# Written-out orders, one-pass scores, and tokens placed pair by pair in a gated cross-attention and routed-FFN kernel

## The chip, the cores and the metric

The kernel runs on one core of one Trainium2 chip. The metric is the device time of one execution in microseconds; lower is better. PE is TensorE, PEld its weight loads, DVE is VectorE, ACT is ScalarE, POOL is GpSimd, SP is SyncE, which here only issues DMAs.

## The reference

`x` is 8 batches of 256 tokens of width 256, the context is 8 batches of 77 keys of width 192. All data are fp32.

```python
# attention, 16 heads of 16
q = layernorm(x) @ wq + bq ; k = y @ wk + bk ; v = y @ wv + bv
out = softmax(q k^T / sqrt(16)) v  @ wo + bo
x = x + tanh(g_xattn) * out
# feed-forward on xf = layernorm(x)
top1 = argmax(softmax(xf @ gate_w.T))            # one of 2 experts per token
h = relu(einsum('end,edh->enh', masked, w1) + b1)  # masked: xf where chosen, else 0
routing_output = (einsum('enh,ehd->end', h, w2) + b2).sum(experts)
shared = relu(xf @ sw1 + sb1) @ sw2 + sb2        # hidden 1024
x = x + tanh(g_ffn) * (routing_output + shared)
```

A token that an expert was not chosen for still adds relu(b1) @ w2 + b2 of that expert: the kernel calls this row `other_row`.

## The kernel before, in words

**Arithmetic.** Most products are made in three fp32r matmuls (`cut`, line 1110 on): each operand is split into a part `hi` that fp32r holds and a rest `lo`, and hi·hi, lo·hi and hi·lo are accumulated. ACT writes `hi` from PSUM, and DVE (for weights in part POOL) writes `lo` as the difference. Scores, values and the product with the probabilities are plain fp32 matmuls, which the trace shows as two records each.

**Attention of one batch** (256 tokens, two groups of 8 heads). `in`: PE transposes the normalised rows `xn` to `xnT`. `query`: 12 fp32r matmuls of 256 columns. `scores`: four quarters (a tile of 128 tokens by a group); each is two fp32 matmuls of 308 columns against `k_diag`, a block-diagonal matrix in which SP has set each head's keys with a DMA of its own (line 409, 8 per batch). `soft`: DVE takes the maxima over 77 keys and subtracts them, in two halves; `exp` is ACT's, `sums` DVE's sum and reciprocal, and POOL multiplies (line 582). `turn`: 20 transposes of the probabilities. `values`: 10 fp32 products with the block-diagonal `v_diag`, which SP fills with 12 small DMAs per batch from DRAM (line 416). `out`: 12 fp32r matmuls; DVE adds to `x_all` and takes the statistics of the second layer norm.

**Shared layers of a pair of batches** (512 tokens). `norm2` transposes the normalised rows, `gate` and `gate_turn` give the two gate scores. For each of 8 chunks of the hidden width, `h` is 6 matmuls of 512 columns, evicted twice by ACT (`hT_hi`, and `h32` from which DVE makes `hT_lo`, line 1006), and `y` is 12 matmuls of 256 columns that accumulate in `y_ps`.

**Order.** `START`, `ORDER` and `END` (lines 86 to 124) list steps (name, pair offset, batch of the pair, k); every engine walks the same list and does its own part of each step. `START` serves pair 0, a hardware loop does `ORDER` for pairs 1 and 2, `END` pair 3. The shared layers of pair i-1 stand among the attention of pair i; those of pair 3 come last. SP has its own program: loads, diagonals, `fill` of `sorted_dram` with 10 DMAs of empty rows (line 477), expert weights.

**Routing.** After the last gate, `count`, `choose` and `sort` give each of the 2048 tokens a row of `sorted_dram`, expert 0 from the front and expert 1 behind a seam at a multiple of 256. POOL then issues 16 indirect DMAs (line 612), one for each 128 tokens. `other` (line 1332) makes `other_row`, 24 matmuls per expert. SP loads the first 256 sorted rows, PE transposes them (line 1340), and nine routed tiles follow in a loop: 8 hidden chunks and 8 output chunks each, a gather of the shared result from `part_dram`, and two scatters to `out`.

The matmuls of `cut` and `mm` all bear line 1114 in the trace.

## Time and profile before

| | us |
|---|---|
| median of 3 runs | 403.01 |
| lowest, highest | 402.02, 403.04 |
| span of the profiled execution | 400.4 |
| PE busy | 355.8 (89%) |
| DVE busy | 241.8 (60%) |
| ACT busy | 186.7 (47%) |
| POOL busy | 162.4 (41%) |
| mean granted TensorE clock | 0.972 |

The profile shows one execution, from its first to its last instruction; no device time is given for that execution by itself, so its span stands beside the three runs. A matmul's own length in the trace contains its way through the array, and neighbours overlap; how far apart two start is what one costs. Several operations share a helper's line, so the tile names tell more than the lines.

### The profile page before, as it was taken

Reading aid. Unit: us, or ns where it says so; the run is one execution under the profiler, and the core shown is the slowest. Engines: PE = TensorE matmul, PEld = TensorE weight load, DVE = VectorE, ACT = ScalarE, POOL = GpSimd, SP = SyncE. Lnnn points to the kernel's source line nnn. Section 1 sums busy time; section 2 is a strip of 40 time slices with the busy share of each in tenths; the row PEclk is TensorE's granted clock in tenths of the full one; section 3 lists DMA queues with packets and bytes.
Section 4 is the critical chain, followed back from the end, with each engine's and each line's share of the span. In section 5 each row is a group of like instructions: output and inputs, shape, how many; then the busy total and the mean of one; then the engine's idle time right before and its main releaser. Section 6 shows DMA issues by size and latency. Waiting matters only on the chain. (4 is left out here: it accounts for less than half of the span.)

```text
span 400.4 us, 7423 instructions
## 1 busy us (share of the span) xinstructions
PE 355.8 (89%) x2341; PEld 313.7 (78%) x2341; DVE 241.8 (60%) x592; ACT 186.7 (47%) x398; POOL 162.4 (41%) x164
## 2 busy tenths in 40 slices
PE   3697868799999999999999999963999999999990
PEld 3475756577889878889868988853999999999990
DVE  0789897669758979668784377640244444445440
ACT  3323544265654346635247238610555456546550
POOL 8132365541612412615026042871244455444452
PEclk9989998999999999999999999995899999999997
DMA  6810170059500030000300012723211222221120
GB/s 157 262 25 10 37 237 12 8 148 249 149 9 11 3 108 12 9 4 4 106 2 0 2 54 58 283 94 118 52 50 43 66 79 69 58 64 43 61 63 10
DMA packets 34541, 28.31 MB, mean 71 GB/s; under 512 B 15562, under 2 KB 32073, under 8 KB 34521
## 3 DMA queue, kind: packets, MB, share of 16 engines
q1 hardware_dynamic: 31737, 21.16, 19.3%
q0 software_dynamic: 2784, 6.91, 5.5%
q8 instruction: 10, 0.16, 0.2%
q14 instruction: 10, 0.08, 0.1%
HBM read 16.02 MB, written 9.82 MB: 65 GB/s over the span
## 5 line engine op out<-in xcount | busy, mean ns | idle before, releaser
L1006 DVE TENSOR_TENSOR hT_lo<-h,hT_hi 128x256 fp32r<-128x256 f32 (+1 forms) x104 | 57.5, 555 | 65.5 <-ACT h L686 60.7
L582 POOL TENSOR_TENSOR probs<-probs,rinv 128x616 f32<-128x616 f32 x32 | 40.9, 1282 | 111.9 <-DVE rinv L902 111.9
L683 ACT ACTIVATE hT_hi<-h_ps,vec_cols 128x256 fp32r<-128x256 f32 (+1 forms) x68 | 39.2, 577 | 61.8 <-PE h_ps L1114 55.7
L753 ACT ACTIVATE probs<-probs 128x616 f32<-128x616 f32 x32 | 23.0, 720 | 53.0 <-DVE probs L953 53.0
L1114 PE MATMUL bank<-k_diag,qT 128*128 128x308 f32 x128 | 39.8, 434 | 3.0 <-ACT qT L700 2.2
L1114 PE MATMUL y_ps<-ew_hi,hT_hi 128*128 128x256 f32 x144 | 42.1, 292 | 0.0
L1114 PE MATMUL y_ps<-ew_hi,hT_lo 128*128 128x256 f32 x144 | 40.3, 280 | 0.0
L1114 PE MATMUL y_ps<-ew_lo,hT_hi 128*128 128x256 f32 x144 | 40.2, 280 | 0.0
L1114 PE MATMUL y_ps<-sw_hi,hT_hi 128*128 128x256 f32 x128 | 38.2, 299 | 1.8 <-DVE hT_lo L1006 1.6
L686 ACT ACTIVATE h<-h_ps,vec_cols 128x256 f32<-128x256 f32 (+1 forms) x68 | 39.0, 574 | 0.0
L1114 PE MATMUL bank<-pT,v_diag 128*128 128x256 f32 (+1 forms) x160 | 36.0, 380 | 0.6 <-ACT pT L723 0.5
L1114 PE MATMUL y_ps<-sw_hi,hT_lo 128*128 128x256 f32 x128 | 36.1, 282 | 0.0
L1114 PE MATMUL y_ps<-sw_lo,hT_hi 128*128 128x256 f32 x128 | 36.1, 282 | 0.0
L1114 PEld LDWEIGHTS bank<-pT,v_diag 128*128 128x128 f32 (+1 forms) x160 | 30.2, 190 | 5.9 <-issue 1.5
L645 POOL DMA_INDIRECT out<-final,scatter_token x18 | 18.9, 1050 | 34.3 <-DVE final L1099 21.1
L944 DVE TENSOR_REDUCE smax<-bank 128x4 f32<-128x308 f32 x64 | 27.9, 469 | 6.9 <-PE bank L1114 6.7
L1114 PEld LDWEIGHTS bank<-k_diag,qT 128*128 128x128 f32 x128 | 22.9, 193 | 9.6 <-ACT qT L700 2.4
L723 ACT ACTIVATE pT<-bank 128x256 f32<-128x256 f32 (+1 forms) x80 | 24.6, 389 | 10.9 <-PE bank L1211 10.9
L1114 PE MATMUL h_ps<-x2T_hi,sw_hi 128*128 128x512 f32 x64 | 27.2, 424 | 0.5 <-ACT h L686 0.5
L1114 PEld LDWEIGHTS y_ps<-ew_hi,hT_hi 128*128 128x128 f32 x144 | 27.1, 188 | 0.6 <-DVE hT_lo L1006 0.2
L953 DVE TENSOR_TENSOR probs<-bank,smax 128x308 f32<-128x308 f32 x64 | 27.4, 470 | 0.1
L1114 PEld LDWEIGHTS y_ps<-ew_lo,hT_hi 128*128 128x128 f32 x144 | 27.2, 189 | 0.0
(168 smaller groups left out, 958.4 us busy)
## 6 DMA issues: line engine op xcount, KB each, us to landing
stage<-in_L_ffn_w SPq DMA_DIRECT2D x4, 1024.0 KB
sorted_dram<-empty_rows SPq DMA_DIRECT2D x10, 257.0 KB, 4.7
xs<-sorted_dram SPq DMA_DIRECT2D x10, 257.0 KB
stage<-in_L_ffn_sw SPq DMA_DIRECT2D x2, 1024.0 KB
xn_all<-xn SPq DMA_DIRECT2D x4, 512.0 KB, 3.7
part_dram<-x_all SPq DMA_DIRECT2D x4, 512.0 KB, 3.0
x_all<-in_x SPq DMA_DIRECT2D x2, 512.0 KB, 9.1
x_all<-in_x SPq DMA_DIRECT2D x1, 1024.0 KB, 12.8
```

Of the source, the lines that this page charges most:

```text
L582: nc.gpsimd.tensor_tensor(pq, pq, rinv[:, b, k, :].unsqueeze(2).to_broadcast([P, HG, KEYS]), ALU.mult).then_inc(p_ready, 1)
L645: pool.indirect_dma_start(out=out[:, :], out_offset=bass.IndirectOffsetOnAxis(ap=scatter_token[:, t:t + 1], axis=0), in_=final[:, t, :], i ...
L683: nc.scalar.activation(hT[0][:, c % HB, 0:width], hidden_bank(c % banks)[:, 0:width], ACT.Relu, bias=b1_sb[:, m, c:c + 1]).then_inc(h_hi, 1)
L686: nc.scalar.activation(h32[:, c % 2, 0:width], hidden_bank(c % banks)[:, 0:width], ACT.Relu, bias=b1_sb[:, m, c:c + 1]).then_inc(h_32, 1)
L723: nc.scalar.activation(pT[0:r, 2 * u + v, :], bank[2 + u % 2][0:r, v * SEQ:(v + 1) * SEQ], ACT.Copy).then_inc(pT_sb, 1)
L753: nc.scalar.activation(probs[:, b, k, :], probs[:, b, k, :], ACT.Exp, scale=HEAD_DIM ** -0.5).then_inc(p_exp, 1)
L944: nc.vector.tensor_reduce(out=smax[:, b, k, half * HH:(half + 1) * HH], in_=by_head(bank[half][:, 0:HALF]), axis=AX_X, op=ALU.max).then_in ...
L953: nc.vector.tensor_tensor(by_head(probs[:, b, k, half * HALF:(half + 1) * HALF]), by_head(bank[half][:, 0:HALF]), m, ALU.subtract).then_in ...
L1006: nc.vector.tensor_tensor(hT[1][:, c % HB, 0:width], h32[:, c % 2, 0:width], hT[0][:, c % HB, 0:width], ALU.subtract).then_inc(h_lo, 1)
L1114: return nc.tensor.matmul(out_, lhsT, rhs, start=start, stop=stop, **kw)
```

## The change

1. The four lists are replaced by five, one for each engine, with every step of all eight batches written out (no loop over pairs). `n` in `tn.b.u.m` and the like: batch (or unit of two batches), part, PSUM bank.
2. Scores of batches 1 to 7 are made with fp32r in one matmul per stack of two heads: the contraction of 128 rows is [q hi; q lo; q hi; q lo] of two heads (32 rows each) against [k hi; k hi; k lo; k lo], block-diagonal over the two heads, 154 columns; four matmuls per quarter. `q_parts` goes to DRAM and comes back in four pieces, the keys in eight. Batch 0 still uses fp32 against a `k_diag`, now made by DVE. Maxima and shift are one DVE instruction per quarter each.
3. `v_diag` is written as rows into a zeroed DRAM image (2 DMAs per batch) and read back whole (2 DMAs, 0.63 MB).
4. Normalising of both layer norms moves from DVE to ACT (`scale`, `bias`), with one more DVE instruction in each root. The `lo` parts of q, k and of 5 of 8 hidden chunks move to POOL.
5. Tokens are placed and scattered per unit of two batches: expert 0 from the front, expert 1 from the back (`flip`), with a running count. POOL issues the scatters of a unit (4) when its places are known.
6. Both `other` products, and the first transposes of sorted rows, stand among the last shared chunks. The bias of the shared layer is added once to `other_row`, and no longer to each row of `x_all`. `fill` comes early on SP.

```diff
-ORDER = [("scores", 0, 1, 0), ("soft", 0, 1, 0), ("exp", 0, 1, 0), ("values", 0, 0, 0), ("norm2", -1, 0, 0),
-         ("scores", 0, 1, 1), ("norm2", -1, 0, 1), ("soft", 0, 1, 1), ("exp", 0, 1, 1), ("norm", 1, 0, 0),
-         ("out", 0, 0, 0), ("gate", -1, 0, 0), ("h", -1, 0, 0), ("scores", 0, 1, 2), ("gate_turn", -1, 0, 0),
...
-CUT_AFTER = {1: (0, 0), 2: (0, 1), 4: (1, 0), 6: (1, 1)}
+LO_ON_POOL = (1, 2, 4, 5, 6)
+PE_ORDER = """
+    yt.0 yt.1 yt.2 yt.3 vt kp.0.0 kp.0.1 kp.1.0 kp.1.1 vp.0 in.0.0 vp.1 vp.2 qy.0.1 in.1.0 vp.3 sc.0.0 qy.1.1
+    sc.0.1 sc.0.2 in.2.0 tn.0.0.1 sc.0.3 tn.0.1.0 qy.2.1 in.3.0 sc.1.0 tn.0.2.1 tn.0.3.0 tn.0.4.1 qy.3.0 sc.1.1
+    in.4.1 sc.1.2 va.0.0 tn.1.0.1 sc.1.3 tn.1.1.1 ou.0.0 sc.2.0 qy.4.1 in.5.0 sc.2.1 tn.1.2.1 tn.1.3.0 tn.1.4.1
+    qy.5.0 sc.2.2 va.1.1 tn.2.0.0 sc.2.3 tn.2.1.0 in.6.1 ou.1.0 qy.6.1 sc.3.0 tn.2.2.0 tn.2.3.1 tn.2.4.0 sc.3.1
+    in.7.1 va.2.0 n2.0.0.1 sc.3.2 n2.0.1.0 qy.7.1 sc.3.3 tn.3.0.0 h.0.0 tn.3.1.0 ga.0.1 sc.4.0 ou.2.0 gt.0.1
+    h.0.1 h.0.2 tn.3.2.1 tn.3.3.0 sc.4.1 h.0.3 tn.3.4.1 ct.0.0 sc.4.2 y.0.0 va.3.1 sc.4.3 h.0.4 tn.4.0.0
+    tn.4.1.1 y.0.1 ou.3.0 sc.5.0 h.0.5 tn.4.2.1 tn.4.3.0 y.0.2 tn.4.4.1 sc.5.1 h.0.6 va.4.0 sc.5.2 y.0.3
+    tn.5.0.1 tn.5.1.0 h.0.7 n2.1.0.1 n2.1.1.0 sc.5.3 y.0.4 y.0.5 ou.4.1 sc.6.0 h.1.0 ga.1.0 tn.5.2.1 h.1.1
+    gt.1.0 tn.5.3.1 sc.6.1 y.0.6 tn.5.4.0 ct.1.1 h.1.2 sc.6.2 va.5.0 sc.6.3 y.0.7 tn.6.0.1 tn.6.1.0 h.1.3 ou.5.1
+    sc.7.0 y.1.0 tn.6.2.0 h.1.4 tn.6.3.1 tn.6.4.0 sc.7.1 y.1.1 va.6.1 sc.7.2 h.1.5 tn.7.0.0 ou.6.1 sc.7.3
+    tn.7.1.0 y.1.2 h.1.6 y.1.3 h.1.7 n2.2.0.1 n2.2.1.0 y.1.4 y.1.5 oth.0.1 h.2.0 tn.7.2.0 h.2.1 y.1.6 tn.7.3.0
+    h.2.2 tn.7.4.0 y.1.7 h.2.3 va.7.0 y.2.0 h.2.4 ou.7.0 y.2.1 h.2.5 ga.2.0 y.2.2 h.2.6 gt.2.0 y.2.3 h.2.7
+    ct.2.0 oth.1.1 n2.3.0.0 y.2.4 n2.3.1.1 y.2.5 y.2.6 h.3.0 ga.3.0 h.3.1 gt.3.1 h.3.2 y.2.7 ct.3.0 h.3.3 y.3.0
+    h.3.4 y.3.1 h.3.5 y.3.2 h.3.6 y.3.3 h.3.7 xst.1 y.3.4 y.3.5 y.3.6 y.3.7
+"""
+POOL_ORDER = """
+    klo.0.0 klo.0.1 bi.0 klo.1.0 va_.0 klo.1.1 bi.1 va_.1 ql.1 di.0.0 bi.2 di.0.1 bi.3 bi.4 di.0.2 di.0.3 ql.2
+    bi.5 di.1.0 ql.3 bi.6 di.1.1 va_.2 di.1.2 di.1.3 bi.7 ql.4 di.2.0 di.2.1 va_.3 ql.5 di.2.2 di.2.3 ql.6
+    di.3.0 di.3.1 di.3.2 ql.7 di.3.3 hl.1 di.4.0 hl.2 scat.0 di.4.1 di.4.2 hl.4 di.4.3 hl.5 di.5.0 hl.6 di.5.1
+    di.5.2 di.5.3 di.6.0 hl.9 scat.1 di.6.1 hl.10 di.6.2 di.6.3 hl.12 di.7.0 di.7.1 hl.13 di.7.2 hl.14 di.7.3
+    hl.17 hl.18 hl.20 wl.5 hl.21 hl.22 scat.2 hl.25 hl.26 scat.3 hl.28 hl.29 hl.30
+"""
+SP_ORDER = """
+    vz kw.0 kw.1 kr.1 qw.1 fl qr.1 vw.0 wd.0 wd.1 kr.2 qw.2 vr.0 vw.1 qr.2 wd.2 wd.3 qw.3 vr.1 vw.2 qr.3 kr.3
+    vr.2 vw.3 qw.4 vw.4 vr.3 qr.4 qw.5 kr.4 qw.6 vw.5 vr.4 qr.5 kr.5 qw.7 vw.6 vr.5 qr.6 kr.6 vw.7 vr.6 qr.7
+    kr.7 vr.7 ps.0 wd.4 wd.5 ps.1 ps.2 xs ps.3
+"""
...
+            def keys_in(b):
+                n = b % 2
+                if b == 1:
+                    sp.wait_ge(cleared[0], 1)
+                else:
+                    sp.wait_ge(s_ready, 4 * (b - 1))
+                sp.wait_ge(k_out[b // 4], 16 * 2 * STACKS)
+                for piece in range(4):
+                    for h in range(2):
+                        to = slice(piece * SR + h * HEAD_DIM, piece * SR + (h + 1) * HEAD_DIM)
+                        sp.dma_start(k_stack[to, n, :, :, h, :].rearrange("r i g n -> r (i g) n").bitcast(F32),
+                                     k_dram[h * HEAD_DIM:(h + 1) * HEAD_DIM, piece // 2, :, :,
+                                            b * KEYS:(b + 1) * KEYS].rearrange("r i g n -> r (i g) n")
+                                     ).then_inc(k_in[n], 16)
+            def queries_out(b):
+                sp.wait_ge(q_hi, b + 1)
+                sp.wait_ge(q_lo, b)
+                if b >= 3:
+                    sp.wait_ge(q_in[b % 2], 16 * 4 * ((b - 1) // 2))
+                sp.dma_start(q_dram[b % 2].rearrange("m p g s -> p m (g s)"),
+                             q_parts[:, :, :, :].rearrange("p m g s -> p m (g s)").bitcast(F32)
+                             ).then_inc(q_out[b % 2], 16)
+            def queries_in(b):
+                n = b % 2
+                if b >= 2:
+                    sp.wait_ge(s_ready, 4 * (b - 1))
+                sp.wait_ge(q_out[n], 16 * ((b + 1) // 2))
+                for piece in range(4):
+                    sp.dma_start(q_stack[piece * SR:(piece + 1) * SR, n, :, :, :].rearrange("r i g s -> r i (g s)"
+                                                                                            ).bitcast(F32),
+                                 q_dram[n, piece % 2].rearrange("(i r) g s -> r i (g s)", i=STACKS)
+                                 ).then_inc(q_in[n], 16)
+            def values_out(b):
+                n = b % 2
+                sp.wait_ge(v_rdy, b // 2 + 1)
+                if b < 2:
+                    sp.wait_ge(v_zeroed, 16 * 4)
+                else:
+                    sp.wait_ge(v_in[n], 16 * 2 * (b // 2))
+                for g in range(GROUPS):
+                    diagonal = bass.AP(v_rows, n * GK * GROUPS * P + g * P,
+                                       [[GROUPS * P, KEYS], [KEYS * GROUPS * P + HEAD_DIM, HG], [1, HEAD_DIM]])
+                    sp.dma_start(diagonal, v32[:, (b // 2) % 2, n, g * P:(g + 1) * P].rearrange("k (h f) -> k h f", h=HG)
+                                 ).then_inc(v_out[n], 16)
+            def values_in(b):
+                n = b % 2
+                sp.wait_ge(v_out[n], 16 * GROUPS * (b // 2 + 1))
+                if b < 2:
+                    sp.wait_ge(v_zeroed, 16 * 4)
+                else:
+                    sp.wait_ge(o_ps, b - 1)
+                full = CHUNKS - 1
+                sp.dma_start(v_diag[:, n, 0:full, :, :].rearrange("p c g f -> p c (g f)"),
+                             v_dram[n, 0:full * P].rearrange("(c p) g f -> p c (g f)", p=P)).then_inc(v_in[n], 16)
+                sp.dma_start(v_diag[0:ROWS[full], n, full, :, :].rearrange("p g f -> p (g f)"),
+                             v_dram[n, full * P:GK].rearrange("p g f -> p (g f)")).then_inc(v_in[n], 16)
...
+            def queries_lo(b):
+                pool.wait_ge(q_32, b)
+                pool.wait_ge(q_hi, b + 1)
+                if b >= 2:
+                    pool.wait_ge(q_out[(b - 1) % 2], 16 * (b // 2))
+                nc.gpsimd.tensor_tensor(q_parts[:, 1, :, :].rearrange("p g s -> p (g s)"),
+                                        q32[:, :, :].rearrange("p g s -> p (g s)"),
+                                        q_parts[:, 0, :, :].rearrange("p g s -> p (g s)"), ALU.subtract
+                                        ).then_inc(q_lo, 1)
...
+            def scatter(u):
+                n, tiles = u % 2, UNIT_TILES[u]
+                pool.wait_ge(numbers_made, 2)
+                if u == 0:
+                    pool.wait_ge(k_lo, 2 * GROUPS)
+                if u >= 2:
+                    pool.wait_ge(scattered[n], 16 * TILES_AS[u])
+                nc.gpsimd.tensor_copy(xn2[:, n, 0:tiles, DIM:ROW].rearrange("p t o -> p (t o)"),
+                                      number[:, TILE0[u]:TILE0[u] + tiles]).then_inc(tokens_put, 1)
+                if u == 0:
+                    pool.wait_ge(filled, 16 * (RTILES + 1))
+                pool.wait_ge(tokens_put, u + 1)
+                pool.wait_ge(xn2_ready, u + 1)
+                pool.wait_ge(places_rdy, u + 1)
+                for t in range(tiles):
+                    pool.indirect_dma_start(
+                        out=sorted_dram[:, :], out_offset=bass.IndirectOffsetOnAxis(ap=place_int[:, n, t:t + 1], axis=0),
+                        in_=xn2[:, n, t, :], in_offset=None, bounds_check=SLOTS - 1,
+                        oob_is_err=False).then_inc(scattered[n], 16)
...
+            nc.gpsimd.memset(part[:, :, :], 0.0).then_inc(part_clear, 1)
+            pool.wait_ge(other_scaled, 1)
+            nc.gpsimd.tensor_tensor(other_row[:, :, :], other_row[:, :, :],
+                                    bias_rows[:, 1, :].unsqueeze(1).to_broadcast([P, EXPERTS, DIM]), ALU.add
+                                    ).then_inc(other_rdy, 1)
...
-                            dve.wait_ge(s_ps, quarter * 2 + half + 1)
-                            nc.vector.tensor_reduce(
-                                out=smax[:, b, k, half * HH:(half + 1) * HH], in_=by_head(bank[half][:, 0:HALF]),
-                                axis=AX_X, op=ALU.max).then_inc(s_max, 1)
+            def maxima(b, k):
+                dve.wait_ge(s_ready, 4 * b + k + 1)
+                nc.vector.tensor_reduce(out=smax[:, b % 2, k, :].rearrange("p (n h) -> p n h", n=2), in_=score_heads(),
+                                        axis=AX_X, op=ALU.max).then_inc(s_max, 1)
+            def shifted(b, k):
+                if b == 1 and k == 0:
+                    dve.wait_ge(k_out[0], 16 * 2 * STACKS)
+                    dve.wait_ge(k_out[1], 16 * 2 * STACKS)
+                if b >= 2:
+                    dve.wait_ge(pT_ps, TURNS * (b - 1))
+                dve.wait_ge(s_max, 4 * b + k + 1)
+                m = smax[:, b % 2, k, :].rearrange("p (n h) -> p n h", n=2).unsqueeze(3).to_broadcast([P, 2, HH, KEYS])
+                nc.vector.tensor_tensor(probs[:, b % 2, k, :].rearrange("p (n h k) -> p n h k", n=2, k=KEYS),
+                                        score_heads(), m, ALU.subtract).then_inc(s_shifted, 1)
...
+                dve.wait_ge(rank_step, 5 * u + 3)
+                dve.wait_ge(counts_ps, u + 1)
+                nc.vector.tensor_tensor_scan(running[:, 1:tiles + 1], bank[m][:, 128:128 + tiles], zero_tile[:, 0:tiles],
+                                             running[:, 0:1], ALU.add, ALU.add).then_inc(rank_step, 1)
+                dve.wait_ge(rank_step, 5 * u + 4)
+                nc.vector.tensor_tensor(rank1[:, 0:tiles], bank[m][:, 64:64 + tiles], running[:, 0:tiles], ALU.add
+                                        ).then_inc(rank_step, 1)
+                dve.wait_ge(rank_step, 5 * u + 5)
+                if u >= 2:
+                    dve.wait_ge(scattered[u % 2], 16 * TILES_AS[u])
+                nc.vector.tensor_tensor(place_int[:, u % 2, 0:tiles], slot0[:, 0:tiles], rank1[:, 0:tiles], ALU.subtract
+                                        ).then_inc(places_rdy, 1)
...
+            let_go = [None, (vecs_rdy, 1)]
+            def fill_bank(m, sem_, count):
+                if let_go[m]:
+                    pe.wait_ge(*let_go[m])
+                let_go[m] = (sem_, count)
...
-                        for half in range(2):
-                            if not early or (b, k) != (0, 0):
-                                pe.wait_ge(s_shifted, quarter * 2 - 1 + half)
-                            mm(bank[half][:, 0:HALF], qT[:, b, g, t * P:(t + 1) * P],
-                               k_diag[:, b, g, half * HALF:(half + 1) * HALF], True, True).then_inc(s_ps, 1)
+            def scores(b, k):
+                t, g = k % TB, k // TB
+                quarter = 4 * b + k
+                if quarter == 0:
+                    pe.wait_ge(yT_sb, 2)
+                    pe.wait_ge(q_hi, 1)
+                else:
+                    pe.wait_ge(s_shifted, quarter)
+                if b == 0:
+                    pe.wait_ge(k_diag_rdy, g + 1)
+                    for half in range(2):
+                        ins = mm(s_ps[:, half, 0:HALF], qT[:, g, t * P:(t + 1) * P],
+                                 k_diag[:, g, half * HH:(half + 1) * HH, :].rearrange("p h k -> p (h k)"), True, True)
+                else:
+                    if k == 0:
+                        pe.wait_ge(q_in[b % 2], 16 * 4 * ((b + 1) // 2))
+                        pe.wait_ge(k_in[b % 2], 16 * 8 * ((b + 1) // 2))
+                    for i in range(STACKS):
+                        ins = mm(s_ps[:, i // 2, i % 2 * SK:(i % 2 + 1) * SK],
+                                 q_stack[:, b % 2, i, g, t * P:(t + 1) * P],
+                                 k_stack[:, b % 2, i, g, :, :].rearrange("p h k -> p (h k)"), True, True)
+                ins.then_inc(s_ready, 1)
...
+            def other(e, m):
+                if e == 0:
+                    fill_bank(m, other_scaled, 1)
+                pe.wait_ge(rb_cut, 1)
+                pe.wait_ge(w_lo[3 + 2 * e], 1)
+                for c in range(HC):
+                    ins = cut(bank[m][:, e * DIM:(e + 1) * DIM],
+                              lambda n: relu_b1p[n][:, e, c:c + 1].to_broadcast([P, P]),
+                              lambda n: ew2_sb[e][n][:, c, :], c == 0, c == HC - 1)
+                ins.then_inc(other_ps, 1)
...
+                if step == "xst":
+                    fill_bank(at[0], xsT_lo, 1)
+                    sorted_turn(0, *at)
+            pe.wait_ge(w_lo[2], 1)
+            pe.wait_ge(w_lo[4], 1)
+            pe.wait_ge(other_scaled, 1)
+            pe.wait_ge(y_out, len(UNITS))
+            pe.wait_ge(h_32, CHUNKS_SHARED)
+            pe.wait_ge(seam_rdy, 1)
+            tiles_of_0 = pe.value_load(tiles0_int[0:1, 0:1], min_val=1, max_val=RTILES - 1)
```

## Rows read from the trace of the kernel before

**Rows 1.** Stretches: length, busy of PE, PEld, DVE, ACT, POOL, clock, DMA share, GB/s
```profile
24.39:92.49 68.10, 57.13 (x299) 43.53 (x298) 54.47 (x157) 28.42 (x59) 31.77 (x26) 0.97 0.30 79
92.49:265.09 172.60, 168.77 (x1036) 144.61 (x1034) 124.74 (x278) 88.57 (x168) 61.70 (x55) 1.00 0.21 60
265.09:283.07 17.98, 8.69 (x56) 8.49 (x55) 2.10 (x3) 0.60 (x1) 5.84 (x6) 0.72 0.31 96
283.07:400.40 117.33, 106.95 (x901) 106.11 (x899) 48.97 (x108) 61.38 (x154) 52.32 (x54) 0.98 0.19 56
```

**Rows 2.** Timeline of SP, its DMA issues: start, us, what
```profile
27.57 20.05 SPq L416 DMA_DIRECT2D v_diag<-values_dram  x24
84.69 6.86 SPq L477 DMA_DIRECT2D sorted_dram<-empty_rows  x10
93.95 1.95 SPq L409 DMA_DIRECT2D k_diag<-kT  x1
```

**Rows 3.** Timeline of PE in the beginning: start, us, what
```profile
19.65 0.55 PE L1114 MATMUL bank<-xnT_hi,wqo_hi 128*128 128x256 f32 x1 [3.74 <-DVE xnT_lo L868]
24.39 1.20 PE L1114 MATMUL bank<-k_diag,qT 128*128 128x308 f32 x4
25.43 1.89 PE L1114 MATMUL h_ps<-wv_sb,yT 96*77 96x256 f32 x8
47.47 4.56 PE L1114 MATMUL bank<-pT,v_diag 128*128 128x256 f32 x20
87.84 1.20 PE L1114 MATMUL bank<-k_diag,qT 128*128 128x308 f32 x4
```

**Rows 4.** Timeline of POOL, first and last of 16 scatters
```profile
247.13 2.74 POOL L612 DMA_INDIRECT sorted_dram<-xn_all,place_int  x1 [8.97 <-issue]
271.74 0.97 POOL L612 DMA_INDIRECT sorted_dram<-xn_all,place_int  x1 [0.30 <-issue]
```

**Rows 5.** The chain that ended last, in order of time
```profile
271.74 2.53 DMA sorted_dram<-xn_all,place_int
274.28 2.96 DMA xs<-sorted_dram
278.40 4.68 PE bank L1114 x24
```

**Rows 6.** Timeline of PE and of DVE at the end of the shared layers
```profile
265.09 0.28 PE L1114 MATMUL bank<-ew_hi,relu_b_hi 128*128 128x256 f32 x1
265.20 0.28 PE L1114 MATMUL bank<-ew_hi,relu_b_lo 128*128 128x256 f32 x1
265.29 1.41 DVE L1015 SCALAR_TENSOR_TENSOR x_all<-y_ps,gains,x_all 128x512 f32<-128x512 f32 x2 [1.78 <-PE y_ps L1114]
```

**Rows 7.** Timeline of PE, paces in the middle of the kernel
```profile
101.37 0.40 PE L1114 MATMUL h_ps<-x2T_hi,sw_lo 128*128 128x512 f32 x1
101.61 0.39 PE L1114 MATMUL h_ps<-x2T_lo,sw_hi 128*128 128x512 f32 x1
107.86 1.04 PE L1211 MATMUL bank<-ident,probs 128*128 128x128 f32 x8
149.47 0.40 PE L1259 MATMUL bank<-ident,gate_rows 2*128 2x2 f32 x4
```

**Rows 8.** Groups of instructions, shapes apart: busy, mean ns, idle before
```profile
L944 DVE TENSOR_REDUCE smax<-bank 128x4 f32<-128x308 f32 x64 | 27.9, 469 | 6.9 <-PE bank L1114 6.7
L899 DVE TENSOR_REDUCE rsum<-probs 128x8 f32<-128x616 f32 x32 | 25.0, 782 | 2.7 <-ACT probs L753 2.7
L902 DVE RECIPROCAL rinv<-rsum 128x8 f32<-128x8 f32 x32 | 6.5, 203 | 1.1
L582 POOL TENSOR_TENSOR probs<-probs,rinv 128x616 f32<-128x616 f32 x32 | 40.9, 1282 | 111.9 <-DVE rinv L902 111.9
L639 POOL TENSOR_TENSOR part<-part,other_row 128x256 f32<-128x256 f32 x18 | 14.9, 846 | 15.9 <-DMA part<-part_dram,gather_token 15.9
```

**Rows 9.** DMA issues: KB each, median us to landing
```profile
xn_all<-xn SPq DMA_DIRECT2D x4, 512.0 KB, 3.7
```

1638 lines of the change are left out of this document (877 added, 761 removed), and 7 rows, old and new, of the table END.

## The prediction, made before the changed kernel ran

> **What bounds it now.** I cut the span at the events of TensorE: the first shared hidden matmul (92.49), the first matmul of `other` (265.09) and the routed part (283.07) [rows 1]. Before 92.5 us TensorE is not the limit: DVE is busy 54.5 of the 68.1 us after the first scores, and SP spends 20.05 us on issuing the 24 pieces of `v_diag`; the first product with `v_diag` (47.47) starts as that ends [rows 1 to 3]. From 92.5 to 265.1 TensorE is busy 168.8 of 172.6 us: there only less work for it helps. From 265.1 to 283.1 it mostly waits. The chain of waits runs through POOL, whose 16 scatters go from 247.13 to 272.7, their landing (2.53), the load of `xs` (2.96), and a cold half of `other`: 24 matmuls in 4.68, at a mean clock of 0.72 in this stretch, against 0.117 apart warm [rows 1, 4 to 6]. From 283.1 on nine routed tiles fill TensorE.
>
> **Paces, warm.** What a matmul costs is the distance to the next one, not its own length. fp32r: 256 columns 0.117 us, 512 columns 0.24; a transpose (1.04 - 0.28)/7 = 0.11 [rows 6, 7]. An fp32 product of 308 columns is two records, and a quarter (two products) goes from 24.39 to 25.43: 1.04 us. The 20 records with `v_diag` are (4.56 - 0.38)/19 = 0.22 apart, 4.4 a batch [rows 3].
>
> **Part 1, scores in one pass.** No row has an fp32r matmul of 154 columns. The line through 256 and 512 columns gives 0.07 us, four per quarter 0.29: 0.75 less than 1.04. The other end is that narrow ones run at the fp32 price per column, 4 x 154 x 1.04/616 = 1.04, and save nothing. I take 0.29, since that line passes near zero, and keep 1.04 for a rival. Loading the weights could be a floor, but `gate_turn` loads 128 columns four times with its matmuls (0.40 - 0.20)/3 = 0.07 us apart [rows 7]. The Trainium skill ("TensorE: Matmul & The Clock Gate", LDWEIGHTS) puts such a load at its columns over 1.2 GHz, 107 ns; the row speaks against that as a distance, and by the rule a quarter would cost 0.43 and the sum come out 2.2 us higher.
>
> DVE now takes the maxima of a quarter in one instruction, not two: 2 x 0.469 become about 0.82 (the 616-wide sum takes 0.782); the shift I price the same. A quarter is 0.82 + 0.82 + 0.78 + 0.20, with gaps 2.8 us [rows 8]. The price is a detour. Per batch ACT evicts the queries twice, POOL subtracts (512 wide: 1.1 us, between 0.85 for 256 and 1.28 for 616), SP writes 512 KB (3.7 to landing, by `xn_all`), reads 1 MB back in four pieces and the keys in eight; the values cost 4 issues instead of 12. At 20.05/24 = 0.84 an issue, 17 replace 20 [rows 2, 8, 9]. Behind 92 us I cost the detour at nothing: between qy.5 and sc.5.0 TensorE has over 30 us of other work. In the beginning it has no such cover.
>
> **Part 2, the beginning.** (a) All four value steps precede the first scores: 24 fp32 records more, 5.3 us, of which the idle 3.74 before `xnT_lo` hides most. Scores start near 26, not 24.39 [rows 3]. (b) Batch 0, still fp32: four times about 3.0, and 4 us for the second root and three `xnT_lo`: 42. (c) Batch 1 needs its stack. qy.1 ends near 29, ACT 2.6, POOL 1.1, qw.1 0.7: 33.5. The ten fills come next on SP: 6.86 us of issues, 2.57 MB, and the queue is slow until 94, 9.3 us after they begin [rows 2]. qr.1 reads its 1 MB behind them: 47. (d) va.0 stands before sc.1.3 and needs vr.0, which SP reaches behind wd.0 and wd.1 (2 MB, at the fills' rate 6.5 to 7.5), kr.2 and qw.2 (5 together), with 0.63 MB of its own (2): 61. With va.0's 4.4 and the last quarter batch 1 ends at 68. (e) Batch 2: 11.2 + 1.4 (two `xnT_lo`) + 0.7 (`oT_lo`) + 1.5 (`x1`, statistics) = 14.8: 83. Batch 3: the same with 2.6 for the root, less its tail: 98. So h.0.0 starts at 98 where it was 92.49. Bounds: 88 if the waits of (c) and (d) are half as long, 112 if each also delays the next stack.
>
> **Part 3, the full stretch.** By 92.49 the old kernel has done half of batch 3's scores [rows 3] and the queries of four batches. At h.0.0 the new order has done two quarters more (2.1), four `in` and `qy` more (4 x 1.84 = 7.4, from 12 x 0.117 and 4 x 0.11) and four transposes (0.4), and lacks ou.2 and ga.0 (2 x 1.4): 7.1 ahead. Of 172.6 remain 172.6 - 7.1 - 16 quarters x 0.75 (12.0) + 5.6 for both `oth` (48 x 0.117), which move in here: 159.1. A check from below: 32 x (6 x 0.23 + 12 x 0.117) = 89 for h and y, scores 4.6, transposes 10, va 21.7, ou 8.4, gates and x2T 9.3, oth 5.6: 149, and 5% for gaps: 157. The others stay below: DVE about 95 of 159 us; POOL takes 20 of 32 `hT_lo` (1.1 each) beside 16 divisions of 1.28 [rows 8]; ACT takes over the normalising, 0.5 a tile.
>
> **Part 4, the handover.** Twelve of sixteen scatters are now issued earlier, under matmuls; four are left after pl.3. From ct.3 to xst TensorE has five h and four y, 12.6 us. Against that: DVE's placing 1, POOL's four issues 5 to 6, landing 2.5, load 3.0 [rows 4, 5]: 12, so xst waits 0 to 1. After y.3.7 it waits for ad.3 (1.41, plus signals) [rows 6]. I take 2.5 for the stretch that took 17.98; cold `other` is gone with it. Four placings instead of one cost DVE some 4 us, beside matmuls.
>
> **Part 5, the routed tiles.** The same instructions per tile; the bias moved from `x_all` into `other_row`, once, under the handover. 117.3 stays [rows 1].
>
> **The sum.** 98 + 159.1 + 2.5 + 117.3 = 376.9 of span against 400.4. The median of the runs shown, 403.0, lies 2.6 above the profiled span; with it **379.5 us**.
>
> **Rivals.** (A) Narrow fp32r matmuls cost what fp32 does, so the change gives no one-pass time: 16 x 0.75 = 12.0 in part 3 (in the beginning it hides under DVE's 0.98 of sums): 391.5. For: no row under 256 columns. Against: the straight line. (B) The beginning is as quick as DVE allows, h.0.0 at 88: 369.5. For: before the stretch SP's queue was its limit, and it issues less. Against: the fills now come early. (C) The last scatters come late: the first of a group takes 2.74, not 0.97 [rows 4], POOL arrives late from its `hT_lo`, TensorE cools: +6, 385.5. (D) Slower than before: SP's single order. Reads of values wait for a va two batches earlier, and stack reads stand behind them. If sc.b.0 or va.b waits t in batches 3 to 7, it costs 5t; above t = 4.7 the time passes 403. With 7, what (d) exposes at batch 1, it is 414.5. For: the fills show a queue full for 9 us [rows 2]; the Trainium skill ("DMA: Bandwidth & Descriptors", Queues, rings and completion order) has each ring consume its descriptors in order. Against: later TensorE has matmuls between, and no block of 2.5 MB follows.
>
> **Chances.** Forecast (own range 371 to 388) 0.50; A 0.25; B 0.12; C 0.06; D 0.05; a mixture near no change 0.02. The range goes from B's side, 366, to A with a late beginning, 397; beyond lie D and the far ends. Within 0.3%, about what a measurement of this kernel cannot tell from no change: 0.02; faster 0.93, slower 0.05.
>
> **What would show it.** Score matmuls 0.07 apart (A: 0.26). The first h at 98, with TensorE's waits before it at sc.1.0 behind the queries' DMA and at va.0 behind the values'. From there to the routed part 162. No wait on `xs` over 1 us; scatters in four groups. Routed part 117. I am wrong if TensorE waits over 10 us in the middle stretch, or if the routed tiles change.

## The result, and the profile after

| | before | after |
|---|---|---|
| median of 4 runs, us | 403.02 | 413.39 |
| lowest, highest | 402.02, 403.10 | 412.10, 415.53 |
| span of the profiled execution | 400.4 | 411.0 |
| mean granted TensorE clock | 0.972 | 0.936 |

The ratio is 1.026, with a 95% interval of 1.022 to 1.030: the change made the kernel slower, where 379.5 us and faster were forecast, and outside the forecast's range of 371 to 388.

The stretches of after, cut at TensorE's first scores, the first stacked scores (`sc.1.0`), the first shared hidden matmul (`h.0.0`) and the routed part (length; busy of PE, PEld, DVE, ACT, POOL; clock; DMA share; GB/s):

```profile
0.00:32.72 32.72, 18.30 (x85) 13.55 (x86) 19.27 (x56) 12.39 (x27) 19.41 (x40) 1.00 0.64 184
32.72:60.47 27.75, 11.74 (x57) 8.17 (x56) 14.88 (x45) 11.74 (x24) 14.83 (x17) 0.77 0.89 193
60.47:123.89 63.42, 50.56 (x273) 44.29 (x273) 42.67 (x77) 34.53 (x63) 23.40 (x22) 0.80 0.84 227
123.89:292.32 168.43, 158.91 (x1043) 141.31 (x1042) 101.47 (x206) 87.89 (x147) 76.61 (x62) 0.99 0.31 78
292.32:411.00 118.68, 107.94 (x900) 107.57 (x900) 48.33 (x108) 61.07 (x153) 52.71 (x54) 0.95 0.20 58
```

Against [rows 1]: from `h.0.0` to the routed part 168.4 us for 190.6 (172.60 + 17.98). There the change does what it is for, and 22.2 us are saved; by the prediction's own count (an estimate) 7.1 of them are work that the new order has only moved ahead of `h.0.0`. But `h.0.0` comes at 123.9 for 92.5, 31.4 us later. The routed part takes 1.4 more. In the beginning the granted clock is 0.77 and 0.80 where it was 0.97, and the DMA engines, idle for 70% of that stretch before, are busy for 84 to 89%.

TensorE in the beginning of after (timeline; four of the six rows from `sc.1.0` to `h.0.0` that have a wait over 1 us ahead of them, in square brackets, and one quarter at full clock with what follows it; the other two waits, 1.28 and 1.89 us, are for VectorE's shift):

```profile
60.47 1.11 PE L1361 MATMUL s_ps<-k_stack,q_stack 128*128 128x154 f32 x4 [11.67 <-issue]
73.00 7.22 PE L1361 MATMUL bank<-pT,v_diag 128*128 128x256 f32 x20 [4.17 <-issue]
83.32 0.57 PE L1361 MATMUL s_ps<-k_stack,q_stack 128*128 128x154 f32 x4
83.72 0.32 PE L1361 MATMUL bank<-xnT_hi,wqo_hi 128*128 128x256 f32 x1
101.15 0.66 PE L1479 MATMUL bank<-ident,probs 128*128 128x128 f32 x4 [1.61 <-ACT q_parts L857]
111.13 1.15 PE L1479 MATMUL bank<-ident,probs 128*128 128x128 f32 x8 [2.06 <-ACT q_parts L857]
```

The values of batch 0, 4.56 us for 20 records before [rows 3], take 7.22: in their first 5 us the granted clock is 0.50, half of full speed. SP's issues around the two long waits:

```profile
35.74 4.77 SPq L451 DMA_DIRECT2D k_stack<-k_dram  x8
40.60 0.38 SPq L462 DMA_DIRECT2D q_dram<-q_parts  x1
41.02 7.46 SPq L526 DMA_DIRECT2D sorted_dram<-empty_rows  x10
48.53 2.53 SPq L473 DMA_DIRECT2D q_stack<-q_dram  x4
51.16 2.52 SPq L489 DMA_DIRECT2D v_rows<-v  x2
53.78 6.19 SPq L518 DMA_DIRECT2D stage<-in_L_ffn_sw  x2
```

and the landings of the queries that stand in the chain of waits:

```profile
64.37 6.05 DMA q_dram<-q_parts
74.29 10.94 DMA q_dram<-q_parts
95.15 5.00 DMA q_dram<-q_parts
104.08 6.04 DMA q_dram<-q_parts
```

`qe` is ScalarE's eviction of a batch's queries into `q_parts`. There is one `q_parts` for all batches, so the next `qe` waits for each of these landings, and what is queued behind `qe` on ScalarE holds TensorE's banks: that is the releaser `ACT q_parts` above. The late start has another source (ScalarE's timeline):

```profile
8.20 0.42 ACT L787 ACTIVATE pT<-s_ps 96x308 f32<-96x308 f32 x1 [2.76 <-PE s_ps L1384]
15.16 0.20 ACT L977 ACTIVATE gains<-gains 128x2 f32<-128x2 f32 x1 [6.54 <-DMA h<-in_L_ffn_b]
15.27 0.40 ACT L787 ACTIVATE pT<-s_ps 96x308 f32<-96x308 f32 x1
```

The tanh is second in `ACT_ORDER` and waits for the expert biases, which take 10.2 us to land; three evictions of the turned context, from which the keys are made, stand behind it.

### The profile page after: what moved, and what is told of

Its sections match the earlier page's. It is cut to its first block, busy times and chain, and to the rows that moved or that the text cites. A ratio compares the mean times of both kernels' runs of the same rounds, so it can differ in the third digit from the quotient of the medians.

```text
span 411.0 us, 7156 instructions
## 1 busy us (share of the span) xinstructions
PE 347.4 (85%) x2353; PEld 314.9 (77%) x2353; DVE 226.6 (55%) x490; ACT 207.6 (51%) x412; POOL 187.0 (45%) x194
## 4 chain that ended last, share of the span: by engine, by line
PE 52%; SPq 11%; DVE 10%; DMA 9%; POOL 6%; issue 6%; ACT 4%; POOLq 0%; DVEq 0%; ACTq 0%
PE y_ps L1361 20%; PE h_ps L1361 14%; PE s_ps L1361 7%; PE bank L1361 7%; DMA q_dram<-q_parts 7%; SPq L451 3%; SPq L473 3%; DMA h<-in_L_ffn_b 2%; PE bank L1479 2%; SPq L526 2%; SPq L518 2%; POOL sorted_dram L691 2%; POOL probs L672 1%; DVE rstd L1042 1%; DVE rsum L1161 1%
## 5 line engine op out<-in xcount | busy, mean ns | idle before, releaser
L1327 DVE TENSOR_TENSOR hT_lo<-h,hT_hi 128x256 fp32r<-128x256 f32 x72 | 32.7, 454 | 48.8 <-ACT h L1021 44.3
L700 POOL TENSOR_TENSOR hT_lo<-h,hT_hi 128x512 fp32r<-128x512 f32 x20 | 27.6, 1385 | 42.2 <-ACT h L935 42.0
L1018 ACT ACTIVATE hT_hi<-h_ps,vec_cols 128x256 fp32r<-128x256 f32 x36 | 17.1, 474 | 50.1 <-PE h_ps L1361 47.9
L930 ACT ACTIVATE hT_hi<-h_ps,vec_cols 128x512 fp32r<-128x512 f32 x32 | 21.9, 684 | 33.5 <-PE h_ps L1361 32.9
L1161 DVE TENSOR_REDUCE rsum<-probs 128x8 f32<-128x616 f32 x32 | 25.3, 789 | 20.4 <-ACT probs L864 19.6
L874 ACT ACTIVATE pT<-bank 128x512 f32<-128x512 f32 x40 | 23.4, 598 | 23.4 <-PE bank L1479 23.4
L1143 DVE TENSOR_REDUCE smax<-s_ps 128x8 f32<-128x616 f32 x32 | 24.9, 779 | 13.8 <-PE s_ps L1361 13.4
L1479 PE MATMUL bank<-ident,probs 128*128 128x128 f32 (+1 forms) x160 | 25.9, 300 | 7.6 <-ACT q_parts L857 3.7
L1361 PE MATMUL s_ps<-k_stack,q_stack 128*128 128x154 f32 x112 | 18.9, 293 | 14.8 <-issue 11.7
L1479 PEld LDWEIGHTS bank<-ident,probs 128*128 128x128 f32 (+1 forms) x160 | 19.7, 151 | 12.5 <-ACT q_parts L857 4.3
```

The costliest lines, as they stand in the source:

```text
L700: nc.gpsimd.tensor_tensor(hT[1][:, q % HB, 0:width], h32[:, q % 2, 0:width], hT[0][:, q % HB, 0:width], ALU.subtract).then_inc(h_lo_pool, 1)
L874: nc.scalar.activation(pT[:, 2 * u:2 * u + 2, :].rearrange("p c s -> p (c s)"), bank[m][:, :], ACT.Copy).then_inc(pT_sb, 1)
L930: nc.scalar.activation(hT[0][:, q % HB, 0:width], h_ps[:, q % 2, 0:width], ACT.Relu, bias=b1_sb[:, 0, c:c + 1]).then_inc(h_hi, 1)
L1018: nc.scalar.activation(hT[0][:, c % HB, 0:RTOK], hidden_bank(c % 4)[:, 0:RTOK], ACT.Relu, bias=b1_sb[:, 1 + e, c:c + 1]).then_inc(h_hi, 1)
L1143: nc.vector.tensor_reduce(out=smax[:, b % 2, k, :].rearrange("p (n h) -> p n h", n=2), in_=score_heads(), axis=AX_X, op=ALU.max).then_inc( ...
L1161: nc.vector.tensor_reduce(out=rsum[:, b % 2, k, :], in_=probs[:, b % 2, k, :].rearrange("p (h k) -> p h k", k=KEYS), axis=AX_X, op=ALU.add ...
```

## The experiments

Each group of kernels ran beside the kernel before on one chip; ratios are to that. Besides the ratio the table gives three points of each profile. `h.0.0` less `sc.1.0` is three batches; "middle" is from `h.0.0` to the routed part. A profile is one execution: `sc.1.0` differs by up to 2.4 us between kernels whose edits don't touch what stands ahead of it.

The expectations number their theories: (1) what stands ahead of the query stacks in SP's order, (2) the round trip of the queries through DRAM as such, (3) the late tanh, (4) VectorE's cut in the last root, (5) the cuts of the shared weights, (6) TensorE is the bound only behind `h.0.0`, (7) the low clock. Step names in the lists: on SP `kw`, `qw`, `vw` write keys, queries and values to DRAM, `kr`, `qr`, `vr` read them back, `fl` is the fills, `wd` a load of weights (0 and 1 shared, 2 and 3 the first expert's), `vz` the zeroing; `wh` and `wl` are ScalarE's and VectorE's parts of cutting weights, `ro` the steps of a reciprocal root, `ad` an addition of the shared result, `kb` matmuls without use, `sm`, `ss`, `su`, `ex` maxima, shift, sums and exponential of the scores, `te` the eviction of turned probabilities; on TensorE `in`, `qy`, `sc`, `tn`, `va`, `ou` are the steps of a batch's attention.

| kernel | ratio (95%) | `sc.1.0` | `h.0.0` | middle |
|---|---|---|---|---|
| after | 1.026 (1.022 to 1.030) | 60.5 | 123.9 | 168.4 |
| fills_late | 1.031 (1.028 to 1.035) | 50.2 | 125.1 | 169.9 |
| tanh_late | 1.017 (1.013 to 1.021) | 56.2 | 118.8 | 169.5 |
| experts_late | 1.025 (1.020 to 1.030) | 60.1 | 123.3 | 169.9 |
| no_detour3 | 1.011 (1.007 to 1.015) | 58.2 | 115.8 | 168.5 |
| fills_first | 1.000 (0.997 to 1.004) | 49.5 | 111.9 | 169.5 |
| cut_late | 1.015 (1.012 to 1.018) | 56.1 | 117.9 | 167.0 |
| pool_writes | 1.025 (1.022 to 1.028) | 56.0 | 119.3 | 171.1 |
| keys_merged | 1.014 (1.010 to 1.018) | 54.7 | 116.8 | 168.6 |
| combined | 0.995 (0.991 to 0.999) | 50.4 | 111.9 | 167.4 |
| shared_cut_later | 0.996 (0.992 to 1.000) | 49.8 | 110.7 | 167.2 |
| shared_load_later | 0.999 (0.995 to 1.003) | 49.5 | 111.3 | 168.6 |
| combined_no_detour | 0.989 (0.986 to 0.992) | 49.5 | 111.9 | 168.9 |
| scores_twice | 1.009 (1.005 to 1.013) | 48.3 | 108.8 | 174.9 |
| kept_busy | 1.005 (1.001 to 1.008) | 49.0 | 114.1 | 168.4 |
| kept_busier | 1.036 (1.029 to 1.043) | 51.2 | 127.1 | 166.9 |
| twice_early | 0.991 (0.988 to 0.994) | 48.0 | 109.9 | 168.5 |
| busy_in_idle | 0.985 (0.979 to 0.990) | 49.6 | 105.9 | 167.0 |
| both_early | 0.993 (0.989 to 0.996) | 48.3 | 110.1 | 168.4 |

**1. What stands in front.** Three orders and one omission, each alone on after.

```diff
 SP_ORDER     # fills_late
-    vz kw.0 kw.1 kr.1 qw.1 fl qr.1 vw.0 ...
+    vz kw.0 kw.1 kr.1 qw.1 qr.1 vw.0 ... vr.3 fl qr.4
 ACT_ORDER    # tanh_late
-    yte.0 tanh yte.1 ...
+    yte.0 yte.1 ... k32.0.0 tanh wohi ...
 SP_ORDER     # experts_late
-    ... qr.2 wd.2 wd.3 qw.3 ...
+    ... qr.2 qw.3 ... qr.6 wd.2 ... qr.7 wd.3 ...
 SP_ORDER     # no_detour3
-    (qw.b and qr.b of b = 3 to 7, and the waits for them)
```

> Only the order of SP is changed: the ten fills of the sorted rows (2.57 MB, 7.5 us of issues) are issued behind the fourth batch's v_diag instead of ahead of the first read of the query stacks. Theory 1 (the queue: what stands ahead of the query stacks in SP's order and in the rings holds the first batches): sc.1.0 comes 8 to 12 us earlier than 60.5, the first shared h 5 to 12 us earlier than 124.1, total 403 to 408. Theory 2 (the round trip through DRAM costs its time whatever stands ahead of it, since q_parts has one buffer): sc.1.0 is earlier, but the first shared h gains under 3 us, total 410 to 413. Theory 3 (the late start by the tanh): as theory 2.

> Only the order of ScalarE is changed: the tanh of the gains, which waits for the 10.2 us load of the expert biases, stands behind the first key eviction instead of second. Theory 3 (the start is lost there): first scores near 28 instead of 32.7 and the total 3 to 5 us down, 408 to 410. Theory 1 (the queue decides from the first stacks on): first scores earlier, but sc.1.0 stays within 1 us of 60.5 and the total within 1 us of 413.

> Only the order of SP is changed: the two loads of the first expert's weights (2 MB), which stand ahead of the third write of the queries, are issued behind the stacks of batches 6 and 7. Theory 1 (traffic ahead of the query round trips): the third and fourth landings of q_dram (10.9 and 5.0 us) fall to about 4, the first shared h 4 to 8 us earlier, total 406 to 410. Theory 2 (round trip as such): within 2 us of 413; and if the weights then come late for the experts' cuts, the handover to the routed layer grows instead.

> From batch 3 on the queries are neither written to DRAM nor read back as stacks: 7.5 MB less traffic and no wait of ScalarE, GpSimd or TensorE for it; the scores of those batches multiply the stacks of batches 1 and 2 again, so the output is another. Theory 2 (the round trip is the price): batches 3 to 7 run at the pace of their engines, first shared h at 105 to 112, total 393 to 400. Theory 1 (what stood ahead of the first stacks): batches 1 and 2 keep their delay, sc.1.0 stays at 60.5, and the total falls by under 8 us, to 405 to 411.

fills_late brings `sc.1.0` 10.3 us forward, and loses all of it before `h.0.0`. The fills now stand not only before `qr.4` but also before `qw.5`, a write of queries; its landing takes 11.49 us, ScalarE's next `qe` waits for it, and TensorE stands 12.59 us in the middle of batch 3 (SP's issues, the chain of waits, TensorE's timeline):

```profile
89.44 7.18 SPq L526 DMA_DIRECT2D sorted_dram<-empty_rows  x10
99.24 11.49 DMA q_dram<-q_parts
111.72 1.97 PE L1479 MATMUL bank<-ident,probs 128*128 128x128 f32 x8 [12.59 <-ACT q_parts L857]
```

So theory 1 holds for its place and fails for its remedy: here too the 2.57 MB cost about 10 us, now behind a write of the queries instead of before a read of them. tanh_late confirms theory 3 for 5.1 us at `h.0.0` (its first scores start at 28.99). The expert weights cost nothing that can be told apart. no_detour3 has `h.0.0` 8.1 us earlier, and nothing changed behind it (168.5 for 168.4). Of the 8.1, 2.3 stand at `sc.1.0`, ahead of all that it leaves out; its three batches take 57.6 us for 63.4. The ratios differ by 0.0150, 6.0 us.

**2. A free place for the fills, and the other suspects**, each on top of tanh_late.

```diff
 SP_ORDER     # fills_first
-    vz kw.0 kw.1 kr.1 qw.1 fl qr.1 ...
+    vz fl kw.0 kw.1 kr.1 qw.1 qr.1 ...
 DVE_ORDER    # cut_late
-    ... ro.3.0 ro.3.1 wl.4 ro.3.2 ...
+    ... ro.3.0 ro.3.1 ro.3.2 ... ad.2 wl.4 ...
 queries_lo   # pool_writes: no qw on SP
+    pool.wait_ge(q_lo, b)
+    pool.dma_start(q_dram[b % 2]..., q_parts...).then_inc(q_out[b % 2], 16)
 keys_out     # keys_merged
-    for m in range(2):
-        sp.dma_start(k_dram[:, m, i, :, cols], k_parts[rows, m, :, cols])
+    sp.dma_start(k_dram[:, :, i, :, cols], k_parts[rows, :, :, cols])
```

> The kernel of tanh_late (408.4 us), with the ten fills issued ahead of the key writes, where SP had nothing to issue from 17.7 to 24.1 us, instead of between the first write of the queries and their read. Theory 1a (what costs is SP's 7.5 us of issues and 2.57 MB at a place where a batch waits for its stacks, and a free place exists): sc.1.0 5 to 8 us earlier than 56.2 and kept, total 401 to 405. Theory 1b (the rings are loaded throughout the first 125 us, and 2.57 MB cost the same wherever they stand, as fills_late suggested with its gain of 10 us given back at the fills' new place): keys and first stacks are late instead, total 407 to 411.

> The kernel of tanh_late (408.4 us), with VectorE's cut of 128x2048 expert weights (2.3 us) moved from among the steps of the last unit's reciprocal root to behind the third addition. Theory 4 (that cut, and the 4.6 us in which VectorE's next small step waited while GpSimd's 5.2 us cut ran, hold TensorE for the 4.3 us of idle time before the last unit's counts): the root ends before GpSimd's cut takes hold, the idle time before the counts falls to under 1.5 us, total 403 to 406. Rival (the handover waits for VectorE's cut in any place, or GpSimd's cut still blocks the small steps): within 1.5 us of 408.4.

> The kernel of tanh_late (408.4 us), with the seven writes of the queries issued by GpSimd, right behind its own cut of them, on its own queue instead of in SP's order. Theory 1 (the writes land late, 5 to 11 us, because they stand behind other steps in SP's order and behind its rings): landings of q_dram fall to 3 to 4 us, the first shared h 5 to 10 us earlier than 118.8, total 398 to 404. Theory 2 (the DMA engines, busy to 86% of the stretch, are the limit, whichever queue): landings stay at 5 us and more, total within 3 us of 408.4 or above, GpSimd's issue of 0.6 to 1 us each added.

> The kernel of tanh_late (408.4 us), with the key writes in 8 transfers of twice the size instead of 16. Theory 1c (SP's issues are what is serial from 24 us on: 16 took 11.5 us, 0.72 each): the key writes take about 6 us, sc.1.0 is 4 to 6 us earlier than 56.2, total 404 to 407. Rival (the issues are slow because the rings are full, so that half as many take as long): sc.1.0 within 1 us of 56.2, total 407 to 410.

fills_first is the largest single gain, 0.0165 of 402 or 6.6 us, all of it at `sc.1.0` (6.7 us): theory 1a. SP's hole there is smaller than the fills, though: 17.7 to 24.1 us in after, 16.6 to 20.3 in tanh_late, and the fills take 8.92. The key writes start 6.3 us later (26.64 for 20.34), take 8.87 us for 11.56, and `qr.1` still goes out at 42.80 for 44.85, since no fill stands between the write of the queries and its read. keys_merged gives 1.5 us at `sc.1.0`, a third of what was expected and less than two profiles can differ by. pool_writes loses: the landings are no shorter (5.8 us in the median, 5.4 with SP). So another queue does not help; that the load on the DMA engines (busy 85% of those batches) stretches the landings is the half of the test that stands, and is argued.

cut_late gives 2.5 us in the middle of its profile (the totals' intervals overlap, so this gain is not clear of noise), and its timelines of VectorE and GpSimd show why not more:

```profile
235.39 0.16 DVE L1044 TENSOR_TENSOR nt<-nt,rstd 128x4 f32<-128x4 f32 x1
235.59 4.47 DVE L1045 SCALAR_TENSOR_TENSOR nt<-nt,rstd 128x4 f32<-128x4 f32 x1
240.09 1.21 DVE L1046 SCALAR_TENSOR_TENSOR rstd<-nt,rstd 128x4 f32<-128x4 f32 x1
```
```profile
235.41 4.62 POOL L706 TENSOR_TENSOR ew_lo<-stage,ew_hi 128x2048 fp32r<-128x2048 f32 x1 [2.64 <-ACT ew_hi L944]
240.00 1.28 POOL L699 TENSOR_TENSOR hT_lo<-h,hT_hi 128x512 fp32r<-128x512 f32 x1
```

A step of 4 columns, 0.16 us by itself, lasts until GpSimd's instruction has ended (240.03), twice in a row. In after it was `rstd`, 4.58 us, against GpSimd's 5.22. The Trainium skill ("SBUF — State Buffer", SBUF: two separate sides) has the two engines share a port pair as an exclusive lock for a whole instruction, on VectorE's side for steps with two inputs in SBUF or in a 2-port mode; these rows agree. TensorE's wait before the last unit's counts fell from 4.3 to 2.1 us, where under 1.5 was expected.

**3. Together, and the order of the shared weights.** combined is tanh_late, fills_first, keys_merged, experts_late and cut_late; the others build on it.

```diff
 ACT_ORDER, DVE_ORDER   # shared_cut_later
-    ... te.0.4.1 wh.0 wh.1 q32.3.0 ...      ... ss.1.1 wl.0 wl.1 su.1.1 ...
+    ... te.2.1.0 wh.0 ... ex.2.3 wh.1 ...   ... su.2.3 wl.0 ... su.3.0 wl.1 ...
 SP_ORDER               # shared_load_later: this, and
-    ... vw.0 wd.0 wd.1 kr.2 ...
+    ... vw.0 kr.2 ... qr.2 wd.0 wd.1 ...
                        # combined_no_detour: shared_cut_later and no_detour3
```

> Five edits of order together: the tanh later, the fills ahead of the key writes, the key writes in 8 transfers, the expert weights' loads behind the last stacks, VectorE's expert cut behind the third addition. If their gains add (fills_first stands at 401.2; the key writes gave 2.4, the cut 1.9, the weights' loads 0.6 by medians): 396 to 398. If the key writes' gain was only room for the rings that the fills already gave back, and the cut's gain needs the late batches to be the limit: 399 to 402.

> The kernel of combined, with the two cuts of the shared weights moved on ScalarE and VectorE from batch 1 to batch 2 and 3. Theory 5 (in the chain of fills_first ScalarE stands 9 us for the landing of the second shared matrix, with the queries of batch 3 queued behind it): the third write of the queries goes out 3 to 8 us earlier, first shared h 3 to 6 us earlier, total 3 to 5 us under combined. Theory 2 (the batches are held by the round trip, and the cut stood in slack): the cuts now stand in front of the first shared h, total within 1 us of combined or up to 3 above.

> The kernel of shared_cut_later, with the loads of the shared weights (2 MB, 3 to 5 us of SP's issues) moved on SP from ahead of batch 2's keys to behind batch 2's stacks. Theory 1 (bytes ahead of a batch's stacks in the rings are what a batch waits for): the stacks of batch 2 land 3 to 6 us earlier and the total falls by 1 to 4 us. Rival (the same bytes only move to batch 3, as the fills' did in fills_late): within 1 us of shared_cut_later.

> The kernel of shared_cut_later without the writes and reads of the queries from batch 3 on (the scores multiply the stacks of batches 1 and 2 again, so the output is another). Theory 1 (with the order mended the round trip is nearly hidden): under 4 us below shared_cut_later. Theory 2 (the round trip of 1.5 MB a batch with one buffer of parts holds the batches in any order): 7 to 12 us below, as no_detour3 was 7.4 below the changed kernel.

The single gains by ratio (0.0165, 0.0029, 0.0017, 0.0012) from 1.0167 make 0.994; combined has 0.995: within their intervals (0.004 each way) they add, though its median, 399.7 us, lies in the range of the other theory (the kernel before was 0.7 us slower in this group). Moving the shared weights does nothing (theory 5 falls, though the chain of fills_first holds a landing of theirs of 8.95 us). And with the order mended, five batches without the round trip give only 0.7%: theory 2 falls as the main cause. Their `h.0.0` at 111.9 says less: that profile, 401.99 us, is 4.4 above the kernel's median of 397.6, and in its chain stand VectorE's two cuts of the shared weights (2.24 us at 92.49 and 2.16 at 101.27), which shared_cut_later had moved there. Its DMA engines are busy 52% of the three batches and TensorE's clock is 0.83, so the queue is not all that binds them.

**4. The clock.** Between `sc.1.0` and `h.0.0` the granted clock is 0.81 in combined. These kernels add matmuls that do nothing useful on top of combined. (kept_busy has 88 of them and kept_busier 200; the 92 and 208 of the expectations were miscounted.)

```diff
 scores       # scores_twice (b >= 1), twice_early (b = 1 to 3)
-    for i in range(STACKS):
+    for i in [n for n in range(STACKS) for _ in range(2)]:
         ins = mm(s_ps[...], q_stack[...], k_stack[...], True, True)
 PE_ORDER     # busy_in_idle
-    ... in.3.0 sc.1.0 ... sc.1.2 va.0.0 ... tn.2.2.0 tn.2.3.1 ...
+    ... in.3.0 kb.20 sc.1.0 ... sc.1.2 kb.12 va.0.0 ... tn.2.2.0 kb.16 tn.2.3.1 ...
+def keep_busy(n):
+    ...
+    for _ in range(n):
+        mm(y_ps[:, 0, 0:P], ident[:, :], before[:, :], True, True)
```

> The kernel of combined (399.7 us), with each score matmul of batches 1 to 7 issued twice into the same place: 112 more matmuls of 128x154, 0.10 us each at full clock. Theory 6 (TensorE is the bound after the first shared h, and not in batches 1 to 3, where it waits): first shared h within 2 us of 111.9, the rest 5 to 7 us longer, total 404 to 408. Rival (TensorE's time is the bound everywhere): first shared h 6 to 9 us later, total 409 to 413. Second rival (what counts is that TensorE idles and its clock falls): no later or earlier first shared h, total at most 403.

> The kernel of combined, with 92 matmuls of 128x128 without use (0.1 us each at full clock) ahead of TensorE's waits in batches 1 to 3, into y_ps, which is free there: 16 ahead of sc.1.0, 4 ahead of each later quarter, 8 or 12 ahead of the values. Theory 7 (the clock granted, 0.81 between the first stacks and the first shared h, costs there what the shorter scores gave): mean clock in that stretch over 0.9, first shared h 3 to 8 us earlier than 111.9, total 392 to 397. Rival (the batches are bound by the chain through VectorE and ScalarE, whatever TensorE's clock): clock up, but first shared h within 2 us, total 398 to 403.

> The kernel of kept_busy with each count doubled and 4 more ahead of batch 0's quarters, the projections and the first unit's transposes: 208 matmuls, 20 to 40 us of TensorE's time. Theory 7: clock near 1 in that stretch, gain as kept_busy or up to 3 us more, until the added matmuls stand in the way. Rival: they only add, total 402 to 412.

> The kernel of combined (0.995 of the kernel before), with the score matmuls issued twice in batches 1 to 3 only, 48 more. Theory 7 (the low clock is a cause: TensorE's work counts in those batches at half clock, and work that keeps the clock up is free): first shared h at 108 to 110 as in scores_twice, the rest as combined, ratio 0.985 to 0.992. Rival (the 3 us of scores_twice were chance of the DMA queue's order): first shared h at 112 to 115, ratio 0.995 to 1.005.

> The kernel of combined, with 48 matmuls of 128x128 without use ahead of TensorE's three longest idle times in batches 1 to 3 (20 ahead of sc.1.0, 12 ahead of va.0, 16 ahead of the transposes that wait for the fourth write of the queries). Theory 7: they fit into idle time, the work behind them runs at full clock: first shared h 3 to 6 us earlier than 111.9, ratio 0.980 to 0.990. Rival (those waits end by DMA and by the other engines, and what TensorE then does faster is waited for again at the next): first shared h within 1.5 us, ratio 0.992 to 1.000.

> The kernel of combined, with the doubled scores of batches 1 to 3 and the first two groups (20 and 12) of the matmuls without use. Theory 7: at most 2 us under the better of the two, ratio 0.978 to 0.988, clock over 0.9 between the first stacks and the first shared h. Rival: the added work stands in the way, ratio 0.995 to 1.01.

In scores_twice 64 more matmuls behind `h.0.0` cost 7.5 us, 0.117 each, so there every matmul counts (theory 6). Ahead of it 48 more, 5.6 us at that price, made the three batches no longer (60.5 us for 61.5), and `h.0.0` came 3.1 us earlier, 2.1 of them at `sc.1.0`, which they don't touch. The rival that has it 6 to 9 us later is out. But the same 48 also raised the clock of the three batches from 0.81 to 0.89 (twice_early has 0.89 too), so this run does not tell waits that hide them from a clock that pays for them. busy_in_idle does. Between first stacks and `h.0.0`, combined and busy_in_idle (stretches, columns as above):

```profile
50.39:111.88 61.49, 48.79 (x272) 43.11 (x273) 41.96 (x77) 34.88 (x63) 24.43 (x24) 0.81 0.78 200
```
```profile
49.61:105.92 56.31, 48.62 (x331) 43.33 (x330) 41.85 (x77) 34.76 (x63) 23.58 (x24) 0.97 0.84 208
```

59 more records, the same busy time, 5.2 us less: at 0.97 the useful work shrinks from 48.8 us to 42.0, by what the useless takes (2.88 + 3.74). VectorE, ScalarE and GpSimd did the same work in less time, so none of them was the limit. In the timeline of TensorE (two records for each fp32 matmul) the added work fills the idle time:

```profile
45.23 4.63 PE L1358 MATMUL y_ps<-before,ident 128*128 128x128 f32 x40
56.23 2.88 PE L1358 MATMUL y_ps<-before,ident 128*128 128x128 f32 x24
60.42 4.56 PE L1358 MATMUL bank<-pT,v_diag 128*128 128x256 f32 x20 [1.31 <-ACT q_parts L854]
90.22 3.74 PE L1358 MATMUL y_ps<-before,ident 128*128 128x128 f32 x32
```

The values of batch 0 are back at 4.56 us. In combined the same place reads

```profile
62.42 6.55 PE L1359 MATMUL bank<-pT,v_diag 128*128 128x256 f32 x20 [3.00 <-ACT q_parts L855]
```

Of the 6.0 us that `h.0.0` gains on combined, 3.6 are there at the third group's end (94.57 for 98.17), the rest behind it. kept_busy reached 0.97 as well, but put matmuls also where TensorE had work: the 72 behind `sc.1.0` take 72 x 0.23 (two records of 0.116) = 17 us, and the three batches last 65.1 us for 61.5. Idle time and the clock together took up 13 of the 17; the runs do not split them. It also left the third wait, 4.07 us, unfilled. So kept_busy's total is that of its rival (398 to 403), not of theory 7, and kept_busier, with 200, passed its rival's 412. Useless work helps only where TensorE would be idle. twice_early (0.991) is not separable from combined. both_early, without the third group, is no better, and misses its forecast of 0.978 to 0.988: there the third wait leaves TensorE at half clock (8 transposes in 1.97 us, 1.14 in busy_in_idle):

```profile
96.00 1.97 PE L1476 MATMUL bank<-ident,probs 128*128 128x128 f32 x8 [4.61 <-ACT q_parts L854]
```

busy_in_idle beats the kernel before, by 1.0 to 2.1%, and the changed one by 4%: its median is 394.5 us for 401.4 (6 and 16 runs). Its runs spread: four lie between 392.8 and 395.3, two at 398.1 and 398.4, beside both_early's, and the profile is of the fastest. combined ran in another group, so between these two the 1% (0.985 for 0.995) rests on both ratios; their intervals just part (0.990 and 0.991).

## Why the prediction was wrong

The sum was 98 + 159.1 + 2.5 + 117.3; the profile has 123.9 + 168.4 (the second and third term) + 118.7. The step that failed is the first, `h.0.0` at 98, with 25.9 of the 34.1 us: the beginning was priced without the late tanh, for a TensorE at full clock, and with too little for the waits that the change brings there. Of the 25.9, 5.1 go with the tanh and 6.8 with the fills, 6.0 come back when TensorE's idle time is filled, and 7.9 stay open.

**(a), first scores at 26: failed, 32.7.** I counted the four value steps and not what the new ScalarE order puts second: a tanh behind a 10.2 us load. tanh_late takes 3.7 us of it back at the first scores (28.99) and 5.1 at `h.0.0`; 3 us of the start stay open.

**(c), `sc.1.0` at 47: the mechanism right, the size off, 60.5.** The fills stand between write and read of the queries, as said, and TensorE waits 11.67 us. Of the 13.5 us too late, 4.3 go with the tanh and 6.7 with the fills. The last 2.5 are open; the key writes hold 1.5 of them at most.

**(d), (e), 15 us a batch: failed, and no order mends it.** The three batches took 63.4 us where I had 51; with the five edits of order together still 61.5. I built the 15 us from VectorE's instructions and priced TensorE's at their warm distances, "paces, warm", because before the change the clock in that stretch was 0.97 [rows 1]. But the change itself takes TensorE's work out of exactly those batches and puts waits there, and the granted clock fell to 0.80: TensorE's own work, 48.8 us busy at 0.81 in combined, came back onto the path. busy_in_idle, 56.3 us at 0.97, shows the size: 5.2 us, even with 6.6 us (2.88 + 3.74) of its own added work inside. The second thing that the 15 us lack is a term for ScalarE's wait on the landing of each query write, which I took at 3.7 us and gave no term in (e): the four in the chain of after take 5.0 to 10.9, and no_detour3, without those from batch 3 on, ran the three batches in 57.6 us for 63.4. What keeps busy_in_idle 5 us above my 51 is open. The landings of 6.31 and 7.71 us that stand in its chain are a candidate. combined_no_detour, which lacks the second of them, took 62.5 us, but at a clock of 0.83 and with the shared cuts in its chain; the two were not tried together.

**Part 3 and 4, 161.6: 6.8 short.** Stacked scores are 0.10 us apart (83.32 to 83.72 for four), not the 0.07 of my line: 64 x 0.03 = 1.9 us. The Trainium skill ("TensorE: Matmul & The Clock Gate", LDWEIGHTS) puts the load of 128 columns at 107 ns, which I had set aside; the 0.10 us measured is nearer to it than to the line. GpSimd's `hT_lo` takes 1.385 and not 1.1; whether that costs anything is not shown. VectorE's cut in the root of the last unit, and its steps locked out by GpSimd, stand ahead of a wait of 4.3 us before the counts, which no part of mine had; cut_late returned 2.5. The other 2.4 are open. "The detour costs nothing behind 92 us" was right: 168.5 without, 168.4 with it. So was the early placing: no wait on `xs` stands in the chain of after, and parts 3 and 4 together fell by 22 us. Of my 2.5 us of handover, TensorE's wait between the last shared product and the routed part is 3.1.

**Part 5, 117.3: 118.7**, at a clock of 0.95 for 0.98; the same instructions. Not followed further.

**The rivals.** A (fp32 price) is out: 0.10, not 0.26. B and C did not come. D had the sign, with 5 in 100, and not the place: it set the price behind batch 2, at 5t, while no_detour3 finds the price of the round trip wholly ahead of `h.0.0`. The rival that was missing is the one of (e): the change makes TensorE wait, and behind the long waits it runs at half clock.

## What to carry to other kernels

Work taken from TensorE pays where TensorE is the limit; in a stretch of waits it can be given back at once, since the clock falls with the idle time: read the granted clock of a stretch as a term that the change moves, not as a constant. When one engine issues all DMAs from a written-out list, ask of each block which consumer stands behind it, and look in the issuing engine's timeline for a place with no read or write behind it that a batch waits for; a block moved from one full place to another (fills_late) gains nothing. Put the longest early load's consumer last in the order of the engine that feeds the others.

## What was not expected of the hardware

- 48 matmuls without use, in idle time, made the kernel 1% faster than the same kernel without them (0.985 for 0.995); the granted clock of the three batches, a mean over its two levels of 1.2 and 2.4 GHz, rose from 0.81 to 0.97.
- The landing of 512 KB took 3.7 us in the median before [rows 9], and 5.0 to 10.9 for the four in the chain of after, with the DMA engines busy to 84%; another queue did not shorten it.
- A 4-column step of VectorE lasts up to 4.6 us beside one GpSimd instruction.
